# Edge features of the second sum stage: moved from SyncE's DMA queue to ScalarE's, loads two tiles ahead

## What is computed

```python
h = relu(layernorm(x));  x = x + sage_two_convs(h, src, dst)        # mean over in-edges, twice, then layer norm
h = relu(layernorm(x));  x = x + gat(h, src, dst, edge_attr_16)
# inside gat, for every edge and head:
a_edge = einsum((attr_all @ W_edge).reshape(-1, H, C), att_edge)   # 16 features -> 4 numbers for an edge
logits = leaky_relu(a_src[src] + a_dst[dst] + a_edge, 0.2)         # then softmax over the edges of a node
```

## Time and profile before

| | us |
|---|---|
| three timed runs | 3786.36, 3793.0, 3794.58 |
| median | 3793.0 |
| the profiled execution, whole | 3779.88 |
| its span | 3778.0 |
| the stage `product_and_norm` in it, first DMA issue to last `rows` | about 1000 to 1601 |
| the part with edge steps (tiles 0 to 23) | about 1000 to 1255 |

### The profile page before, as it was taken

The page is one execution under the profiler, slowest core; times in us unless marked ns, Lnnn a source line. Parts: engine busy times, 40 slices in busy tenths (PEclk is TensorE's granted clock), DMA queues, the critical chain, the costliest instruction groups (busy, mean ns, idle before and its releaser), DMA issues. The chain is left out here.

```text
span 3778.0 us, 71084 instructions
## 1 busy us (share of the span) xinstructions
PE 3235.5 (86%) x21900; PEld 2590.8 (69%) x21900; DVE 2631.2 (70%) x7500; ACT 1011.2 (27%) x2337; POOL 1916.0 (51%) x1970
## 2 busy tenths in 40 slices
PE   5799889999998899978888888888888888888884
PEld 5567656777754566557777777777777777777773
DVE  4789999995577544466666666666666666666666
ACT  4455545664200111122222222222222221122220
POOL 5520111521002232167777777777777777777770
PEclk7699999999999999966666666666666666666666
DMA  5233324651366788632222222222222222222254
GB/s 166 93 133 151 127 112 149 165 160 70 104 211 197 205 248 233 182 91 55 55 54 55 54 55 54 55 55 54 55 54 55 55 54 55 54 56 54 55 49 108
DMA packets 148908, 382.00 MB, mean 101 GB/s; under 512 B 39270, under 2 KB 83230, under 8 KB 140450
## 3 DMA queue, kind: packets, MB, share of 16 engines
q0 software_dynamic: 61648, 127.82, 17.5%
q1 hardware_dynamic: 55222, 230.15, 17.0%
q10 hardware_dynamic: 31676, 19.47, 1.7%
HBM read 259.00 MB, written 119.89 MB: 100 GB/s over the span
## 5 line engine op out<-in xcount | busy, mean ns | idle before, releaser
L1917 POOL DMA_INDIRECT G<-x_tab,idx x1620 | 1533.8, 947 | 533.7 <-issue 515.3
L2088 DVE TENSOR_TENSOR ACC<-pu,ACC 128x140 f32 x1650 | 486.8, 295 | 400.5 <-issue 252.9
L2000 PE MATMUL pu<-MSG,OH 128*128 128x140 f32 x3300 | 665.2, 358 | 83.0 <-DVE ACC L2088 78.9
L2000 PEld LDWEIGHTS pu<-MSG,OH 128*128 128x128 f32 x3300 | 576.0, 249 | 109.3 <-DVE ACC L2088 102.8
L1989 PE MATMUL px<-ADG,OHT 128*128 128x4 f32 x3270 | 609.2, 313 | 0.0
L1989 PEld LDWEIGHTS px<-ADG,OHT 128*128 128x128 f32 x3270 | 581.0, 270 | 12.1
L911 PE MATMUL psR<-SPL,AE 128*128 128x384 bf16 x3038 | 566.6, 327 | 0.0
L1610 PE MATMUL psR<-SPL,AE 128*128 128x384 bf16 x3038 | 519.9, 331 | 14.9 <-DMA AE<-a_tab 14.9
L878 ACT CAST AE<-psA 128x784 bf16<-128x784 f32 x496 | 398.3, 813 | 332.3 <-PE psA L901 332.3
L1610 PEld LDWEIGHTS psR<-SPL,AE 128*128 128x128 bf16 x3038 | 299.9, 99 | 213.3 <-DMA AE<-a_tab 17.1
L1937 ACT COPY OHT<-pt 128x512 f32<-128x512 f32 (+1 forms) x436 | 238.6, 558 | 688.2 <-PE pt L1976 686.9
(11 more groups left out here) (410 smaller groups left out, 3150.5 us busy)
## 6 DMA issues: line engine op xcount, KB each, us to landing
a_tab<-AE SPq DMA_DIRECT2D x62, 1568.0 KB, 5.7
AE<-a_tab SPq DMA_DIRECT2D x62, 800.0 KB, 6.4
AE<-a_tab SPq DMA_DIRECT2D x62, 768.0 KB, 5.8
G<-x_tab,idx POOLq DMA_INDIRECT x1620
at_in<-in_edge_attr SPq DMA_DIRECT2D x26, 250.0 KB
room<-in_edge_attr SPq DMA_DIRECT2D x24, 250.0 KB
x_tab<-H ACTq DMA_DIRECT2D x13, 264.0 KB, 4.1
x_keep<-X ACTq DMA_DIRECT2D x13, 256.0 KB, 4.2
```

What stands on the lines that cost most here:

```text
L1917: pool.indirect_dma_start(G[:, u % 3, j, :], None, x_tab, bass.IndirectOffsetOnAxis(ap=idx[:, u % 3, j:j + 1], axis=0)).then_inc(s_g[u % 3 ...
L2000: mm = pe.matmul(pu[:, k[0], k[1]:k[1] + MW], OH[:, u % 4, j, :], MSG[:, u % 2, j, :], start=True, stop=True)
L2088: dve.tensor_tensor(a, pu[:, k[0], k[1]:k[1] + MW][:, None, :], a, ALU.add).then_inc(s_c, 1)
```

## The change

At tile `i` SP no longer touches the edge features. ScalarE's queue does: the inputs of steps 0, 1 and 2 before everything else in the stage (so before the loads of the node features), then at tile `i` first the result of step `i-1` out, once DVE has finished that step, and right behind it the input of step `i+2` in. The number of buffers, the bytes and DVE's work stay as they are.

```diff
             @block.sync
@@
                         sp.dma_start(r_tab[o * P:(o + 1) * P], RP[:, o % 2]).then_inc(s_rt, 16)
                         sp.wait_ge(s_rt, 16 * (o + 1))
-                    e = i - 3
-                    if 0 <= e < E_REST:
-                        sp.wait_ge(s_ed, e + 1)
-                        sp.dma_start(aeo[:, (E_FIRST + e) * ES:(E_FIRST + e + 1) * ES, :], ae_o[0:EP, e % 3]
-                                     ).then_inc(s_es[e % 3], 16)
-                    if i < E_REST:
-                        if i >= 3:
-                            sp.wait_ge(s_ed, i - 2)
-                        sp.dma_start(at_in[0:EP, i % 3], attr[:, (E_FIRST + i) * ES:(E_FIRST + i + 1) * ES, :]
-                                     ).then_inc(s_el[i % 3], 16)
             @block.scalar
@@
+                def edges_in(e):
+                    if e >= 3:
+                        act.wait_ge(s_ed, e - 2)
+                    act.dma_start(at_in[0:EP, e % 3], attr[:, (E_FIRST + e) * ES:(E_FIRST + e + 1) * ES, :]
+                                  ).then_inc(s_el[e % 3], 16)
+
+                def edges_out(e):
+                    act.wait_ge(s_ed, e + 1)
+                    act.dma_start(aeo[:, (E_FIRST + e) * ES:(E_FIRST + e + 1) * ES, :], ae_o[0:EP, e % 3]
+                                  ).then_inc(s_es[e % 3], 16)
+
+                for e in range(3):
+                    edges_in(e)
                 load(0)
                 load(1)
                 for i in range(NSL):
+                    if 1 <= i <= E_REST:
+                        edges_out(i - 1)
+                    if 3 <= i + 2 < E_REST:
+                        edges_in(i + 2)
                     for q in range(NQ - 1):
                         if i == ends[q] + 1:
                             norm(q)
```

## The result

The time went from 3785.66 us (median of 7 runs, the three of the table above among them, 3778.34 to 3794.58) to 3766.04 us (7 runs, 3760.64 to 3769.89). The ratio is 0.9939, 95% interval 0.9925 to 0.9953: 23 us, with the interval 18 to 28. The medians are 19.6 us apart.

The account below looks back on a forecast made before the run. PE and DVE were taken to follow SP, late from waiting for its r_tab store. PE 13.4, DVE 4.7 and input wait 5.5 made 23.6 us, less 1 and 0.5: 22 us, 3793 to 3771, range 3766 to 3775 (8 in 10: 3763 to 3784).

Parts of the forecast that it names:

- part 2: SP's queue: edge bytes leave it, the store lands 4.6 us after A2, SP never late; less 1 us for stretched A loads.
- Part 8, the start: Stage start: three inputs on ScalarE's queue compete with the first A loads; bounds nothing to 3.2 us, 0.5 us taken.
- PE starting over 1 us after 1005.3: Sign named in advance that would show the forecast wrong, at PE's first matmul of the stage.
- part 3: PE, tiles 9 to 16: without stalls, tile 17 starts at 1151.4 instead of 1164.85, 13.4 us earlier.
- Parts 1 and 2: SP's queue: two issues a tile leave, 9.2 us of SP's time over 13 tiles, and 250 + 62.5 KB a tile leave.
- only SP's issue time: Rival: bytes cost the same, SP's tile becomes 9.3 us, 19.5 us gained, 3774; partial gains of 8 to 19 us got 0.17.
- the store landing in 4 to 7 us: Sign expected after the change: SP's r_tab store lands within 4 to 7 us.
- the second case of this rival: DVE still waits for inputs, so only the 9.2 us of issue time remain, 3784; partial gains of 8 to 19 us: 0.17.
- DVE on time, 4.7 us: Tile 17: without waiting for inputs, DVE is ready for edges(17) 0.95 us after PE's start instead of 5.65, 4.7 us gained.
- The input wait, 5.5 us: Step 17: its input, issued over 14 us before use, is there, so DVE waits 5.5 us less before edges(17).
- `OVG` hidden: Norm at tile 17: gathered rows arrive at 1151.7 to 1156.2, needed at 1158.4, so hidden with 2 us in hand.
- PE's wait at `psg`, 6.5 us: Middle of tile 18: PE's wait for GE from DVE shrinks from 10.58 to some 6.5 us, DVE setting the pace.

Follow-up runs that it names:

- two_sems: Kernel before, r_tab stores counting on two semaphores, so SP waits before a store for the one two tiles earlier: 4894.44 against 4916.43 us, ratio 0.9956.
- in_on_act: Changed kernel with results back on SP's queue, inputs still on ScalarE's: 4893.79 against 4916.43 us for the kernel before, ratio 0.9947.
- beta_early: Changed kernel with GpSimd's add of the second quarter, L1387, moved ahead of its wait for r_tab: 3762.07 us, one run.
- before_again: The kernel before, unchanged, profiled again beside other experiments; no time given for this profile, GE of tile 18 at 198.48 us from the first A load.
- start_wait_all: Changed kernel, ScalarE waiting for A1 of tile 0 to land before issuing any input: 4893.83 us, beside 4914.6 of the kernel before.
- start_fix: Changed kernel, only the input of step 0 ahead of ScalarE's wait for A1 of tile 0, those of steps 1 and 2 behind: 3764.55 us, one run.
- act_split_in: Changed kernel with each input of 125 rows loaded as 112 and 13 rows: 3769.64 us, beside 3788.72 of the kernel before, one run.

## Where the forecast came out, and which of its steps failed

The forecast was 22 us less and 3771 us; measured were 23 us by the ratio, 19.6 by the medians, and 3766.04. The absolute time came out 5 us under the forecast because the base did: before measured 3785.66 over all its runs, not 3793 (7.3 us less), and the medians' gain was 2.4 us smaller. At `GE`, where the sum was made, the gain was 19.15 us for 22.1.

**The step that failed is part 2**, what comes of the bytes that leave SP's queue. It took the end of its bounds at which the store lands 4.6 us after A2's issue and SP is never late. Measured are landings of 7.4 us in the median for 7.7 (7.3 for 7.6 in the mean of tiles 9 to 16), and an SP that issues A1 5 us later than before already at tile 5 (42.9 for 37.8 from the first A load). The prediction saw that the store's landing holds everything behind it, but put the long landing down to the edge bytes on that queue and expected it to shorten with them; two_sems shows that standing still for it is what costs, with all bytes in place. **Part 8, the start, was mis-sized**: 0.5 us, measured 2.1, and "PE starting over 1 us after 1005.3", which the prediction had named as a sign of being wrong, came true (1007.75). A third term, the product stretched by 1.7 us, stood at nothing.

That the gain came out all the same is in part luck. SP's own work for a tile is now about 0.9 us of issues and 7.3 of landing, 8.2 us (an estimate from the traces' shortest run of three issues and mean landing), against 8.4 to 8.5 of PE: the 13.4 us of part 3 came through by 0.2 to 0.3 us a tile, which the prediction's sum did not contain.

Small slips in its working changed nothing: the store at 1078.37 is that of tile 9, not 8; 19 to 25 us off 3793 are 3768 to 3774, not 3766 to 3775.

1. *Parts 1 and 2: issue time, 9.2 us, and bytes nearly free.* The two issues are gone as forecast. The rival "only SP's issue time" wanted 9.3 us a tile; it was 8.53, so it fell. But "the store landing in 4 to 7 us" was wrong: the first store lets A1 of tile 5 go only 7.5 us later (1035.87 to 1043.38), and A1, A2 and the next store go out within 0.9 us (to 1044.27), so that this store again has both A loads ahead of it. Of the 11.8 us that SP's eight tiles lost, issues are 5.7, landings 2.5 and less waiting for PE 3.6. The 4.5 us are seen in two_sems, which has all bytes on SP's queue but never issues A1 late. The rule of the Trainium skill that was the second case of this rival ("DMA: Bandwidth & Descriptors", "Issuing engines are not separate DMA queues") holds here for the transfers, since one queue reaches the same `GE`; its consequence, that only issue time is saved, does not hold (19 to 23 us for 9.2), since a landing was waited for on that queue.

2. *PE without stalls, 13.4 us.* Held. Tile 8 ended at 1086.5 (83.5 us after the first A load before, 86.06 after) and tile 17 began 68.05 us later; forecast were 67.8. The 1 us allowed for stretched A loads was not needed. Of the 2.55 us by which tile 8 ended later, 2.1 are the start (6).

3. *DVE on time, 4.7 us.* Held: from `rows(16)` to `edges(17)` 0.74 us (forecast 0.94).

4. *The input wait, 5.5 us.* Held: gone. The sum left unnamed that `edges(17)` also needs the landing of the result of step 14; in in_on_act that wait, 4.37 us, stands where the input's stood. The change took the results off the landing too, and so it did not show.

5. *What the sum left out.* The product that begins `edges(17)` took 2.40 us for 0.69, 1.7 us on the path that ends in `GE`. That collision was there before too, in `edges(16)`, hidden by the wait of 5.53 us for the input (DVE, before):

```profile
1166.88 1.91 DVE L1753 TENSOR_TENSOR prod<-room,MB 125x512 f32<-125x512 f32 x1
```

The sum did not ask what the vanished wait had covered. beta_early shows the cause: with the add elsewhere this product takes 0.68 us. The Trainium skill ("GPSIMD Engine Reference", section "Specifications") has it that GpSimd shares its SBUF interfaces with VectorE and contends with VectorE's instructions that have two inputs in SBUF; the product is one, and the trace agrees with 1.91, 2.10 and 2.40 us beside the add for 0.69.

6. *The start, 0.5 us.* Mis-sized: 2.1 us at the first matmul (7.31 us for 5.20) and 2.55 by the end of tile 8. The 7.09 us for 6.37 of the first 30 matmuls are not the inputs' doing: they took 7.88 in before_again and 7.95 in two_sems, which have no input on ScalarE's queue. The prediction had 0 and 3.2 as bounds and chose near the wrong one. start_wait_all shows that the inputs do it, start_fix that the first suffices, act_split_in (6.45) that part of it goes with the form of 125 rows. Where the other 1.1 to 1.3 us come from stays open.

7. *`OVG` hidden.* Held. The first gather began at 1146.01 rather than at 1139.7 to 1144.2, and no wait for it is seen. Four gathers take 3.8 us to the last issue and 6.2 to land, so the rows were there at about 1156 (an estimate from these), some 7 us before L1654 at 1163.18.

8. *PE's wait at `psg`, 6.5 us.* 8.30: the product's 1.7 us, since PE came to tile 18 in time.

Sum at `GE`: 22.1 forecast, less 2.05 for the end of tile 8 (2.55 for 0.5), less 1.7 for the product, plus the 1.0 not needed, makes 19.35; measured 19.15.

That the terms close so well at `GE` is worth no more than the 1 to 4 us by which repeats of a profile move it. two_sems gets the same gain from the wait itself, without the start's 2 us.

## What to carry to other kernels

Where a queue's sequencer waits for its own store to land, everything behind it is late by that landing; look first whether the wait can be put before the store after next (two semaphores), and only then move transfers. Moving part of them gives less than a share when the consumer needs all of them: list what one step waits for, a free output buffer too, since a wait that ends earlier than another shows in no profile until that other is gone. When a wait disappears from a path, look at what it had covered, above all operations that another engine stretches, and price them as visible.

## What was unexpected of the hardware

- A product of DVE (125x512, 0.69 us) took 1.91 to 2.40 us in eleven of the executions here when GpSimd's 128x512 add of 1.27 us began during it, 1.2 to 1.7 us more.
- One input of 250 KB in 125 rows, issued 0.07 us ahead of the first A load on another queue, put PE's start back by 2.1 us; in 112 + 13 rows by 1.2.
- A transfer of 125 rows increments its semaphore 6 times in the traces, one of 128 rows 16 times, a pair of 112 and 13 rows 30 times.
- The form in 112 + 13 rows let the `r_tab` store of another queue land in 5.4 us instead of 7.4 (median).
- The attention stage took 2177 to 2182 us in some executions and 3220 to 3223 in others, with a granted clock of 0.79 to 0.80 and 0.72 to 0.74 over the whole execution, whatever the edit.
